# Masked products by one expert in the first token stage, work moved across the seams between stages, narrower causal masks and another order in the second attention

## The chip, the cores and the metric

One NeuronCore of a Trainium2 chip runs the whole program. The metric is the device time in microseconds of one execution, the median of several. The engines are PE (matmul), DVE (vector), ACT (scalar), POOL (GpSimd) and SP, which here only issues DMAs. In the code `nc.tensor` work is under `@block.tensor`, POOL's under `@block.gpsimd`, and so on.

## What is computed

Two layers, each an attention and a gated expert block on the same normalised input, over 4 batches of 1024 tokens of 128 values. The reference, cut:

```python
# layer 0: xn = layernorm(x); x = x + attention0(xn) * silu(experts0(xn))
scores = (Q K^T + Q rel_emb^T) / sqrt(8)          # 16 heads of 8, relative positions clipped to +-127
out = softmax(scores) V;  out Wo + bo
onehot = one_hot(argmax(xt @ gate_w + gate_b))    # 8 experts, the best one
g = einsum('te,eth->th', onehot, xt @ expert_w + expert_b)
# layer 1: the same frame with
scores = q k^T + causal                            # 16 half heads of 8, -inf above the diagonal
w = attn[:, :, 0] - lam * attn[:, :, 1];  o = rms(w v);  o Wo
hmid = gelu(x w1^T + b1); y = hmid w2^T + b2       # 8 experts, 256 hidden, the best two weighted
```

## The kernel before

The program is four stages: `token_stage(0)`, `attention_stage(0)`, `token_stage(1)`, `attention_stage(1)`. Each stage is one block; at its end all engines meet, and the next stage begins for all. I call them tokens 0, attention 0, tokens 1 and attention 1.

**A token stage** takes 8 groups of 512 tokens. For a group it loads X (POOL issues the DMA, L601 and L638), DVE takes mean and variance (`statistics`, L907 to L912), POOL the reciprocal root by three Newton steps (`scale`, L437 to L454), DVE normalises (`normalise`, L917), PE transposes (L832) and ACT copies to XT (L738). Then come the projections Q, K and V (L837, L845, L850), the router, and the split of Q and K into bf16 parts, whose pieces POOL makes (`parts`, L613 and L616) and SP stores to DRAM. `steps` writes the order out by hand: in eight steps the expert work of group g alternates with the front work of group g+1, and the functions named `body` of all engines walk it in the same order.

The expert work of tokens 0 is masked. PE spreads the one-hot choice of an expert over all partitions (`spread_choice`, L797, a 128x512 matmul with the weight `pick_e`), DVE multiplies it with XT into HM (L1015), and PE multiplies HM with the expert's weight into one accumulating bank (L809). This goes by two experts: two spreads, one product of 1024 columns, eight matmuls. The semaphores are `cb_psum` (spread done), `xm_ready` (product done) and `cb_used` (bank read). In the first group DVE also makes the tables of the attention (`attention_tables`) at the odd experts.

After the eighth expert ACT takes the activation into G (L729), and SP stores G to DRAM (L678). SP ends a token stage by waiting until all its stores have landed, `g_stored` last (L713).

**An attention stage** takes 32 units of 128 queries (8 a batch). Its order on each engine comes from a planner, `attention_plan`: it lists the steps of all units with costs (`COST`) and what they wait for, and takes for each engine, among the steps that could start within `NEAR_BY` ns of the earliest one, the one with the least due time (`AIM`, in units; a step that keeps PE's shape is favoured by `STAY`). Per unit PE makes scores once for the row maxima (`row_scores` L1191 in layer 1, `max` and `near` in layer 0), DVE reduces them (L1448), PE transposes the maxima (L1369), POOL splits them in three bf16 rows, and SP puts these into QS beside the queries (L1208). Then PE makes scores again with the maxima subtracted (`far_scores`, L1178), ACT takes exp (L1306), and PE multiplies with V (L1388). Three double banks are shared by both kinds of scores. In layer 0 the blocks beside the diagonal go through `near_scores` (L1153, L1158), for which POOL first copies the unit's queries from QS into QN and QP (step `perm`, L1255 and L1256).

In layer 1 a block on the diagonal is masked by adding -1e30 with matmuls (`mask_rows`, L1167): the weight is one half of the identity, the moving side one half of the mask's rows, repeated for four heads. A unit has four such masks, two for its maxima and two for its exponentials.

At the start of an attention stage ACT issues the DMAs for the keys of batch 1 (`load_kv`, L473 to L477), and those of batches 2 and 3 after the last output copy of units 7 and 15. POOL loads the residual and G of a unit (L1241, L1242).

## Time and profile before

| | us |
|---|---|
| median of 3 runs | 2071.6 (2067.59 to 2082.31) |
| profiled execution | 2077.91 |
| its span, first to last instruction | 2076.1 |
| PE busy in the span | 1767.2 (85%) |
| DVE busy | 1325.2 (64%) |
| ACT busy | 1195.4 (58%) |
| POOL busy | 1146.4 (55%) |

Busy time is the union of an engine's instructions. Idle time in a row is what stood just before the instruction or group, with the instruction that ended it behind the arrow. The stages follow each other without overlap, so a microsecond taken from one is a microsecond of the program unless a later stage gives it back.

### The profile page before, as it was taken

The numbers are of one execution on the slowest core, as the hardware profiler recorded it, in microseconds if no ns is written. First come the engines' busy times: TensorE is split into PE (matmuls) and PEld (weight loads), VectorE is DVE, ScalarE is ACT, GpSimd is POOL, SyncE is SP. The second block draws the span as 40 slices with busy tenths as digits, with TensorE's granted clock in tenths as the row PEclk, the third lists the DMA queues.
The fourth block names the chain that finished last, engine by engine and source line by source line (L and its number), as shares of the span: only waits on it lengthen the run. The fifth ranks groups of instructions, "written<-read, shape, count | busy, mean of one in ns | idle before, by whom it ended". The sixth has DMA issues, their size and how long they took to land. (4 is left out here: it accounts for less than half of the span.)

```text
span 2076.1 us, 78586 instructions
## 1 busy us (share of the span) xinstructions
PE 1767.2 (85%) x34080; PEld 1327.7 (64%) x34080; DVE 1325.2 (64%) x1965; ACT 1195.4 (58%) x1438; POOL 1146.4 (55%) x1502
## 2 busy tenths in 40 slices
PE   5887489998898998989999759999968978879886
PEld 4666377777777776778877536666735545546554
DVE  5442367777676766877777424445467868867883
ACT  2322167777677766777877623344416645656555
POOL 4742469997699858998898621221112333333433
PEclk9887699999999999999999869999979989979998
DMA  3456312123221241222121121133220131121110
GB/s 104 129 146 191 93 52 66 48 65 96 73 65 59 67 106 60 68 68 59 55 62 55 52 91 53 57 95 88 80 61 18 30 66 26 41 52 30 26 26 16
DMA packets 166300, 139.97 MB, mean 67 GB/s; under 512 B 91715, under 2 KB 157014, under 8 KB 160454
## 3 DMA queue, kind: packets, MB, share of 16 engines
q1 hardware_dynamic: 153370, 105.93, 17.9%
q10 hardware_dynamic: 7212, 16.42, 3.3%
q0 software_dynamic: 5376, 12.59, 2.2%
q8 instruction: 271, 4.44, 0.9%
q14 instruction: 71, 0.58, 0.1%
HBM read 90.98 MB, written 43.12 MB: 65 GB/s over the span
## 5 line engine op out<-in xcount | busy, mean ns | idle before, releaser
L1306 ACT ACTIVATE a_EX<-bank 128x1024 f32<-128x1024 f32 x624 | 616.1, 1025 | 292.4 <-PE bank L1178 227.4
L1425 DVE TENSOR_TENSOR a_PM<-bank,a_PM 128x1024 f32<-128x1024 f32 x336 | 402.2, 1222 | 169.0 <-PE bank L1178 156.8
L1265 POOL TENSOR_TENSOR a_SN<-a_SN,a_MB 128x1024 f32<-128x1024 f32 x176 | 421.1, 2429 | 46.3 <-DMA a_MB<-m_dram 45.1
L1448 DVE TENSOR_REDUCE a_M<-bank 128x2 f32<-128x1024 f32 (+3 forms) x304 | 340.3, 1165 | 85.5 <-PE bank L1191 54.9
L1388 PE MATMUL bank<-a_EX,VV 128*32 128x128 f32 x9984 | 360.0, 288 | 3.5 <-issue 1.8
L1178 PE MATMUL bank<-QS,KS 51*128 51x128 bf16 (+1 forms) x4992 | 237.9, 230 | 89.5 <-DMA QS<-a_MP 38.1
L1388 PEld LDWEIGHTS bank<-a_EX,VV 128*32 128x32 f32 x9984 | 270.8, 115 | 52.1 <-issue 22.9
L1178 PEld LDWEIGHTS bank<-QS,KS 51*128 51x128 bf16 (+1 forms) x4992 | 160.1, 100 | 183.1 <-issue 57.6
L1302 ACT ACTIVATE a_SN<-bank 128x1024 f32<-128x1024 f32 x176 | 177.2, 1026 | 93.6 <-PE bank L1158 92.5
L1310 ACT ACTIVATE a_SN<-a_SN 128x1024 f32<-128x1024 f32 x176 | 185.4, 1058 | 38.8 <-POOL a_SN L1265 38.5
L1158 PE MATMUL bank<-QP,rel_t 112*128 112x32 bf16 x5632 | 197.7, 177 | 1.4 <-issue 1.2
L1158 PEld LDWEIGHTS bank<-QP,rel_t 112*128 112x128 bf16 x5632 | 170.5, 97 | 2.0 <-issue 1.9
L1153 PE MATMUL bank<-QN,KS 112*128 112x64 bf16 x2816 | 142.6, 194 | 27.7 <-POOL QP L1256 20.7
L1026 DVE SCALAR_TENSOR_TENSOR t_ACC<-bank,t_C,t_ACC 128x128 f32<-128x128 f32 x256 | 72.1, 345 | 147.4 <-PE bank L825 146.4
L1178 PE MATMUL bank<-QS,KR 48*128 48x128 bf16 (+1 forms) x2688 | 126.1, 229 | 38.0 <-DVE a_PM L1425 15.7
L825 PEld LDWEIGHTS bank<-t_w,t_HM 128*128 128x128 f32 x1024 | 122.1, 192 | 47.2 <-ACT t_HM L723 29.5
L1191 PE MATMUL bank<-KS,QS 48*128 48x128 bf16 (+3 forms) x1152 | 117.3, 288 | 34.1 <-DVE a_M L1448 21.7
L1178 PEld LDWEIGHTS bank<-QS,KR 48*128 48x128 bf16 (+1 forms) x2688 | 82.2, 99 | 82.4 <-issue 36.5
L825 PE MATMUL bank<-t_w,t_HM 128*128 128x128 f32 x1024 | 127.2, 278 | 8.4 <-ACT t_HM L723 6.9
L1432 DVE TENSOR_TENSOR a_PM<-a_SN 128x1024 f32<-128x1024 f32 x64 | 106.9, 1671 | 42.2 <-ACT a_SN L1302 36.0
L1256 POOL COPY QP<-QS 48x1024 bf16<-48x1024 bf16 x64 | 131.5, 2054 | 0.0
L1153 PEld LDWEIGHTS bank<-QN,KS 112*128 112x128 bf16 x2816 | 107.2, 98 | 35.7 <-issue 33.4
(151 smaller groups left out, 2487.8 us busy)
## 6 DMA issues: line engine op xcount, KB each, us to landing
a_MB<-m_dram SPq DMA_DIRECT2D x32, 1024.0 KB, 4.9
QS<-q_dram SPq DMA_DIRECT2D x192, 96.0 KB, 3.0
KS<-k_dram ACTq DMA_DIRECT2D x12, 768.0 KB
q_dram<-t_PARTS SPq DMA_DIRECT2D x32, 192.0 KB, 2.8
k_dram<-t_PARTS SPq DMA_DIRECT2D x16, 384.0 KB, 2.9
QS<-a_MP SPq DMA_DIRECT2D x384, 2.0 KB
q_dram<-t_PARTS SPq DMA_DIRECT2D x32, 128.0 KB, 2.6
k_dram<-t_PARTS SPq DMA_DIRECT2D x16, 256.0 KB, 2.9
```

Source lines behind the costliest of these rows:

```text
L825: last = pe.matmul(y, HM[:, k % 2, h, t * P:(t + 1) * P], w2[:, k, h, :], start=h == 0, stop=h == 1)
L1153: pe.matmul(out_b[:, :, 4 * pair:4 * pair + 4], KS[0:KD, it.u // NB % 2, pair, it.jb * P:(it.jb + 1) * P], QN[:, r, pair, q0:q0 + CQ // 2, ...
L1158: last = pe.matmul(out_b[:, i, :], rel_t[:, y:y + P], QP[:, r, q0 + i, :, :].rearrange("k h a -> k (h a)"), start=False, stop=i == CQ // 2 ...
L1178: last = pe.matmul(bank[:, 2 * it.n + hh, k * P:(k + 1) * P], kblock(hh, rows, it.u, it.jb, pair), QS[hh * HALF:hh * HALF + rows, it.u % Q ...
L1256: last = pool.tensor_copy(QP[rows, r, :, :, a], QS[rows, q, :, :, :].rearrange("k p h (q b) -> k q (p h) b", b=2)[:, :, :, a])
L1265: pool.tensor_tensor(near_view(sn), near_view(sn), as_near(MB[:, :, :], it.part), ALU.add)\
L1302: act.activation(near_buffer(u, jb)[:, part, :], src.rearrange("p b c -> p (b c)"), ACT.Copy).then_inc(act_done, 1)
L1306: act.activation(as_banks(EX[:, it.need % ER[layer]], part), by_head, ACT.Exp, scale=SCALE).then_inc(act_done, 1)
L1310: act.activation(sn, sn, ACT.Exp, scale=SCALE).then_inc(nexp_done, 1)
L1388: last = pe.matmul(dst_o, VV[:, u // NB % 2, jb, vo:vo + 32], ex, start=bool(it.first) and h < 4, stop=bool(it.last), skip_group_check=True)
L1425: dve.tensor_tensor(pm, mb.rearrange("p hh (k i) -> p hh k i", k=4), pm, ALU.max).then_inc(max_used, 1)
L1448: dve.tensor_reduce(target.rearrange("p (hh k) -> p hh k", hh=2)[:, :, p0:p0 + g], mb[:, :, 0:g * width].rearrange("p hh (k j) -> p hh k j ...
```

## The change

It has five parts.

1. Tokens 0: the masked products are made by one expert in place of two. A spread, a product of 512 columns and the handshake are each for one expert; the first four spreads of a group are issued in front steps 6 and 7, and expert k issues the spread of expert k + 4.
2. Seam 1: POOL copies the queries of units 0 and 1 (`permute`) at the end of tokens 0. ACT's exponential and DVE's last steps for `lam` move into attention 0.
3. Seam 2: in attention 0 POOL loads the first X of layer 1 and SP its projection weights into a part of KR that is free by then, after unit 28's output; DVE takes the statistics after the output of unit 30, POOL the root before unit 31's addition, and DVE normalises before unit 31's output.
4. The end of both token stages no longer waits for the stores of G; the loads of G in the attention wait for what they read, and the first copy into OS, which now shares its place with G, waits for all stores.
5. Attention 1: a mask is built from tables of 64 shifted key columns in two halves. Each of its four matmuls has 256 columns in place of 512 and writes every second column of its bank. The cost of a mask in the planner falls from 480 to 260, and layer 1 has new due times and windows, so that its order changes. The order of attention 0 stays, but for the moved copies.

The diff, cut to its core:

```diff
-        "mask": 480, "evict": 1028, ...
+        "mask": 260, "evict": 1028, ...
...
-    {"max": (-0.94, 0.96), "mrow": (-5.54, -2.26), "msplit": (-1.51, -3.76), "exp": (1.3, 0.81),
+    {"max": (-0.89, 0.93), "mrow": (-5, -1.11), "msplit": (-2.16, -1.22), "exp": (1.31, 0.71),
...
-NEAR_BY, STAY = (179, 222), (0.55, 1.3)
+NEAR_BY, STAY = (179, 493), (0.55, 0.47)
...
+        spare = KR[:, 0, :, :].rearrange("p a s -> p (a s)").bitcast(F32)
+        X1 = spare[:, 0:512].rearrange("p (t d) -> p t d", d=P)
+        XN1 = spare[:, 512:1536].rearrange("p (c t d) -> p c t d", c=2, d=P)
...
                     parts(GROUPS - 1)
+                    if layer == 0:
+                        for u in range(NR):
+                            permute(pool, u)
...
-                    sp.wait_ge(g_stored, 16 * GROUPS + 1)
...
                     def spread_choice(g, e):
-                        pe.wait_ge(cb_used, g * (E // 2) + e // 2 + 1)
-                        for k in range(2):
-                            last = pe.matmul(bank[:, HB + e % 4 + k, :], pick_e[:, e + k, :], CTB[:, :], start=True, stop=True)
-                        last.then_inc(cb_psum, 1)
+                        pe.wait_ge(cb_used, g * E + e + 1)
+                        pe.matmul(bank[:, HB + e % 4, :], pick_e[:, e, :], CTB[:, :], start=True, stop=True).then_inc(cb_psum, 1)
...
-                            if k % 2 == 0:
-                                if k + 2 < E:
-                                    spread_choice(f, k + 2)
-                                pe.wait_ge(xm_ready, f * (E // 2) + k // 2 + 1)
+                            pe.wait_ge(xm_ready, f * E + k + 1)
+                            if k + 4 < E:
+                                spread_choice(f, k + 4)
...
-                        if kind == "front" and k == 7 and layer == 0:
-                            spread_choice(f, 0)
+                        if kind == "front" and k >= 6 and layer == 0:
+                            spread_choice(f, 2 * (k - 6))
+                            spread_choice(f, 2 * (k - 6) + 1)
...
-                        if kind == "expert" and layer == 0 and k % 2 == 0:
-                            dve.wait_ge(cb_psum, f * (E // 2) + k // 2 + 1)
+                        if kind == "expert" and layer == 0:
+                            dve.wait_ge(cb_psum, f * E + k + 1)
                             if f or k >= 4:
-                                dve.wait_ge(y_psum, f * E + k - 2)
-                            dve.tensor_tensor(HM[:, k // 2 % 2, :, :], bank[:, HB + k % 4:HB + k % 4 + 2, :],
-                                              XT[:, p:p + 1, :].broadcast_to([P, 2, GROUP]), ALU.mult).then_inc(cb_used, 1)
+                                dve.wait_ge(y_psum, f * E + k - 3)
+                            dve.tensor_tensor(HM[:, k // 2 % 2, k % 2, :], bank[:, HB + k % 4, :], XT[:, p, :],
+                                              ALU.mult).then_inc(cb_used, 1)
...
             def mask_rows(pe, it, which):
-                for part in range(2):
+                for half in range(2):
                     for hh in range(2):
                         rows = slice(hh * HALF, (hh + 1) * HALF)
-                        last = pe.matmul(bank[:, 2 * it.n + hh, :].rearrange("p (h c) -> p h c", h=4), mask_b[rows, 0, part, :],
-                                         mask_b[rows, which, part, None, :].broadcast_to([HALF, 4, P]), start=False,
-                                         stop=part == 1, skip_group_check=True)
+                        out_h = bank[:, 2 * it.n + hh, :].rearrange("p (h c a) -> p h c a", h=4, a=2)[:, :, :, half]
+                        last = pe.matmul(out_h, mask_b[rows, which, half * P:(half + 1) * P],
+                                         mask_b[rows, which, None, 2 * P:].broadcast_to([HALF, 4, HALF]), start=False, stop=True,
+                                         skip_group_check=True)
...
                         elif it.kind == "final":
+                            if layer == 0 and u == UNITS - 1:
+                                scale(pool, 1, 0)
...
+                            if layer == 0 and u == UNITS - 4:
+                                pool.wait_ge(av_done, spare_free)
+                                for r in range(2):
+                                    pool.wait_ge(stored[r], 16 * GT // 2)
+                                load_x(pool, 1, dst, X1, 0)
...
+                    if layer == 0:
+                        act.wait_ge(lam_sum, 1)
+                        act.activation(lam_s[:, 0:2], lam_s[:, 0:2], ACT.Exp).then_inc(lam_exp, 1)
...
+                            if layer == 0 and u == UNITS - 1:
+                                normalise(dve, 1, X1, XN1, 0, 0)
...
+                            if layer == 0 and u == UNITS - 2:
+                                statistics(dve, 1, X1, 0)
```

What this makes of PE's order in tokens 0, from the last matmuls of one group's bias (`out_b`) to the values of the next (`t_pick_e` is a spread, `t_exp_w` the matmuls of an expert, `t_XN` the transposition, `t_wq`, `t_wk` and `t_wv` the projections). Before:

```order
L864 MATMUL bank<-out_b,t_CT 128x128 x4
L809 MATMUL bank<-t_exp_w,t_HM 128x128 x4
L797 MATMUL bank<-t_CTB,t_pick_e 128x512 x4
L809 MATMUL bank<-t_exp_w,t_HM 128x128 x4
L832 MATMUL bank<-eye,t_XN 128x128 x4
L809 MATMUL bank<-t_exp_w,t_HM 128x128 x4
L837 MATMUL bank<-t_XT,t_wq 128x512
L840 MATMUL bank<-gate_w,t_XT 128x8 x4
L797 MATMUL bank<-t_CTB,t_pick_e 128x512 x2
L809 MATMUL bank<-t_exp_w,t_HM 128x128 x4
L845 MATMUL bank<-t_XT,t_wk 128x512
L809 MATMUL bank<-t_exp_w,t_HM 128x128 x4
```

After, from the same matmuls on:

```order
L923 MATMUL bank<-out_b,t_CT 128x128 x4
L858 MATMUL bank<-t_CTB,t_pick_e 128x512 x2
L868 MATMUL bank<-t_exp_w,t_HM 128x128 x4
L858 MATMUL bank<-t_CTB,t_pick_e 128x512 x3
L868 MATMUL bank<-t_exp_w,t_HM 128x128 x4
L891 MATMUL bank<-eye,t_XN 128x128 x4
L858 MATMUL bank<-t_CTB,t_pick_e 128x512
L868 MATMUL bank<-t_exp_w,t_HM 128x128 x4
L896 MATMUL bank<-t_XT,t_wq 128x512
L899 MATMUL bank<-gate_w,t_XT 128x8 x4
L858 MATMUL bank<-t_CTB,t_pick_e 128x512
L868 MATMUL bank<-t_exp_w,t_HM 128x128 x4
```

Two spreads have moved ahead of the last expert of the group, and the others stand one by one between the experts; none is left between the values and the fifth expert.

POOL at seam 1, from the last split of Q and K on (the BRANCH rows are the change of stage, `a_XG` the loads of residual and G). Before:

```order
L616 TENSOR_TENSOR t_PARTS<-t_FR,t_PARTS 128x1536
L598 UNCONDITIONAL_BRANCH
L1235 UNCONDITIONAL_BRANCH
L1241 DMA a_XG<-in_x 128x128
L1242 DMA a_XG<-g_dram 128x128
L1241 DMA a_XG<-in_x 128x128
L1242 DMA a_XG<-g_dram 128x128
L1255 COPY QN<-QS 48x512x2
L1256 COPY QP<-QS 48x1024
```

After:

```order
L522 COPY QN<-QS 48x512x2
L523 COPY QP<-QS 48x1024
L665 UNCONDITIONAL_BRANCH
L1275 UNCONDITIONAL_BRANCH
L1282 DMA a_XG<-in_x 128x128
L1283 DMA a_XG<-g_dram 128x128
L1282 DMA a_XG<-in_x 128x128
L1283 DMA a_XG<-g_dram 128x128
L522 COPY QN<-QS 48x512x2
L523 COPY QP<-QS 48x1024
```

The copies of units 0 and 1, four pairs of which the last is shown, now stand ahead of the change of stage; the pair behind the loads is that of unit 2.

PE in attention 1 around the transposed maxima of unit 9 (`eye,a_M`), before the keys of batch 2 are loaded (this load follows the `a_EX,VV` row, the last one of unit 7). Before:

```order
L1369 MATMUL bank<-eye,a_M 16x128
L1178 MATMUL bank<-QS,KS 128x128 x8
L1167 MATMUL bank<-mask_b 128x512 x4
L1178 MATMUL bank<-QS,KS 128x128 x8
L1167 MATMUL bank<-mask_b 128x512 x4
L1191 MATMUL bank<-KS,QS 128x128 x8
L1402 MATMUL bank<-eye,a_OF 128x128
L1191 MATMUL bank<-KS,QS 128x128 x8
L1388 MATMUL bank<-a_EX,VV 32x128 x16
```

After:

```order
L1411 MATMUL bank<-eye,a_M 16x128
L1228 MATMUL bank<-KS,QS 128x128 x8
L1204 MATMUL bank<-mask_b 128x256 x4
L1444 MATMUL bank<-eye,a_OF 128x128
L1228 MATMUL bank<-KS,QS 128x128 x16
L1447 MATMUL bank<-wo,a_OT 128x128
L1228 MATMUL bank<-KS,QS 128x128 x8
L1204 MATMUL bank<-mask_b 128x256 x4
L1430 MATMUL bank<-a_EX,VV 32x128 x16
```

The exponentials' scores of unit 8 (`QS,KS` with their masks) have moved ahead of the transposition, and row scores of the next unit (`KS,QS`) stand in their place.

## Rows read from the trace of the kernel before

**Rows 1.** Busy time by stretch: start:end, length, each engine, then PEclk, DMA share, GB/s.

```profile
core 0: us, PE busy (x) PEld busy (x) DVE busy (x) ACT busy (x) POOL busy (x), PEclk, DMA share, GB/s
0.00:216.00 216.00, 159.65 (x864) 125.50 (x864) 95.86 (x265) 60.72 (x76) 96.42 (x141) 0.83 0.50 142
216.00:1205.00 989.00, 862.85 (x22816) 715.80 (x22816) 681.16 (x608) 699.49 (x784) 790.56 (x528) 0.93 0.23 65
...
1522.00:2076.00 554.00, 460.11 (x8832) 286.46 (x8832) 409.61 (x556) 314.80 (x385) 198.04 (x704) 0.90 0.16 36
```

**Rows 2.** Timeline of PE, a middle group: start, length, instruction, idle before and releaser.

```profile
119.11 1.41 PE L809 MATMUL bank<-t_exp_w,t_HM 128*128 128x128 f32 x8 [0.93 <-DVEq L1017]
...
127.21 1.05 PE L809 MATMUL bank<-t_exp_w,t_HM 128*128 128x128 f32 x8
128.73 1.16 PE L850 MATMUL bank<-t_wv,t_XT 128*128 128x128 f32 x8 [0.47 <-ACT t_FQ L747]
...
132.34 0.82 PE L809 MATMUL bank<-t_exp_w,t_HM 128*128 128x128 f32 x5 [1.92 <-DVEq L1017]
```

**Rows 3.** DVE: three rows of the timeline, one of the groups (count, busy, mean ns).

```profile
28.00 2.62 DVE L985 TENSOR_SCALAR t_rel_r<-t_rel_f 112x766 f32<-112x766 f32 x1
...
127.03 0.22 DVE L956 COPY t_C<-t_OH 128x32 f32<-128x32 f32 x1 [0.38 <-issue]
...
131.02 1.23 DVE L1015 TENSOR_TENSOR t_HM<-bank,t_XT 128x1024 f32<-128x1024 f32 x1 [0.20 <-issue]
...
L925 DVE TENSOR_SCALAR t_FQ<-bank 128x512 f32<-128x512 f32 x16 | 10.9, 683 | 2.2 <-PE bank L845 2.2
```

**Rows 4.** Timeline at seam 1, POOL, ACT, ACT's queue and PE.

```profile
213.32 1.28 ACT L775 ACT_TABLE_LOAD   x1
...
216.59 0.60 POOL L1241 DMA_DIRECT2D a_XG<-in_x  x1 [16.95 <-POOLq L598]
...
219.72 0.47 ACTq L477 DMA_DIRECT2D VV<-v_dram  x1
...
230.22 1.04 POOL L1255 COPY QN<-QS 48x1024 bf16<-48x1024 bf16 x1 [8.51 <-issue]
...
233.28 0.59 PE L1153 MATMUL bank<-QN,KS 112*128 112x64 bf16 x8 [20.69 <-POOL QP L1256]
...
242.63 1.02 ACT L1302 ACTIVATE a_SN<-bank 128x1024 f32<-128x1024 f32 x1 [0.24 <-PE bank L1158]
```

**Rows 5.** Timeline at seam 2, POOL, DVE and PE.

```profile
1205.16 0.77 POOL L601 DMA_DIRECT2D t_X<-x_mid  x1 [2.45 <-POOLq L1198]
...
1208.87 0.87 DVE L907 BATCH_NORM_STATS2 t_stats<-t_X 128x6 f32<-128x128 f32 x4 [6.73 <-DMA t_X<-x_mid]
...
1216.47 1.09 PE L832 MATMUL bank<-eye,t_XN 128*128 128x128 f32 x4 [14.67 <-DVE t_XN L917]
...
1220.74 0.87 DVE L907 BATCH_NORM_STATS2 t_stats<-t_X 128x6 f32<-128x128 f32 x4 [4.42 <-DMA t_X<-x_mid]
```

**Rows 6.** Timeline at seam 3, SP's queue and PE.

```profile
1519.29 0.36 SPq L678 DMA_DIRECT2D g_dram<-t_G  x1
...
1522.24 0.61 PE L1191 MATMUL bank<-KS,QS 48*128 48x128 bf16 x8 [6.10 <-PEq L598]
```

**Rows 7.** The masks: the line's matmuls, the chain's shares, two rows of the timeline.

```profile
L1167 PE MATMUL bank<-mask_b x512: 373/377/631, 1522.6 to 2054.7; 64*128 64x512 bf16 x171
...
by line: DVE a_M L1448 5.9%; issue 3.4%; PE bank L1388 3.3%; PE bank L1178 2.5%; PE bank L1191 1.6%; DMA QS<-a_MP 1.4%; PE bank L1167 1.3%; ACT a_EX L1306 1.0%; DVEq L1494 0.6%; SPq L1208 0.5%; PE bank L1396 0.4%; PE bank L1402 0.4%; PE ban
...
1551.37 0.60 PE L1167 MATMUL bank<-mask_b 64*128 64x512 bf16 x4
1551.80 0.39 PE L1191 MATMUL bank<-KS,QS 48*128 48x128 bf16 x8
```

**Rows 8.** Timeline of attention 1, rows of maxima, keys of batch 2, PE's wait.

```profile
1672.24 4.30 SPq L1208 DMA_DIRECT2D QS<-a_MP  x6
...
1674.12 1.49 ACTq L473 DMA_DIRECT2D KS<-k_dram  x2
...
1688.71 1.04 PE L1178 MATMUL bank<-QS,KS 51*128 51x128 bf16 x16 [8.13 <-DMA QS<-a_MP]
```

More of the change, by code:

```diff
@@ L1112, in attention_stage @@
             AV, MISC = 2 * SLOTS2, 2 * SLOTS2 + 1
+            far_end = max(n for n, it in enumerate(plan["pe"]) if it.kind in ("max", "exp") and it.u < UNITS - NB)
+            spare_free = min(it.k for it in plan["pe"][far_end:] if it.kind == "av") + 1
             def block_of(u):
@@ L1181, in far_scores @@
                 if masked:
-                    last = mask_rows(pe, it, 2)
+                    last = mask_rows(pe, it, 0)
                 return last
```

198 lines of the change are left out of this document (111 added, 87 removed).

## The prediction

> **What bounds the kernel now.** I read the busy time by stage first [rows 1]. The program is four stages in a row, each ended by a barrier of all engines: tokens 0 (0 to 216 us), attention 0 (to 1205), tokens 1 (to 1522) and attention 1 (to 2076). Inside attention 0 PE is busy 862.85 of 989 us at a granted clock of 0.93, and the change leaves its order on PE, ACT and DVE alone, so I expect it to keep its length and only to start sooner. The change works in four places: the expert steps of tokens 0, the three seams between stages, and the masks and the order of attention 1. I take them in this order, from the timeline of each.
>
> **Tokens 0, the products by one expert.** In a middle group PE waits twice for DVE's masked product: 0.93 us before the first expert and 1.92 us before the fifth; the 0.47 us before the values is for ACT [rows 2]. The first wait is the chain spread, product, expert: the spread for experts 0 and 1 is issued right ahead. After the change the spread for 0 and 1 stands one expert earlier, so product 0 is ready before PE asks: -0.9 us. The second wait stands behind DVE's evacuation of the values: product at 131.02, 1.23 us long, PE at 132.34. A product of 512 columns costs about 0.68 us, the mean of the nearest row (a 128x512 operation out of PSUM) [rows 3], so PE starts 0.55 us sooner; but the two spreads that lay in this wait now stand at the group's end, on PE's path, and take about 0.5 us. That is 0. Against this, the product for the fourth expert used to be made with the third, ahead of the routing chain; now it stands behind it. Routing ends at 127.03 + 0.22 = 127.25 [rows 3]; with 0.68 for the product and 0.2 for the handover PE could start this expert at 128.1, where it started at 127.21 [rows 2]. Of these 0.9 us the wait for ACT hides 0.47: +0.4. Sum -0.5 us a group, six groups with this pattern: -3. In the first group four table steps of DVE stand ahead of the odd products; the first of them alone takes 2.62 us [rows 3] and was covered by the product for two experts made before it. Cover gone, I walk through this group and end 1.3 us later. The last group has no front steps; PE runs there without waiting for DVE. Sum: -2 us. Bounds: -8 if fewer stops also lift the clock (0.83 over the stage [rows 1]), +6 if the tables cost their full length.
>
> In rows, the extra work of DVE is 32 more operations: 2 x 0.68 for one of 1.23 is 0.13, and the pause before the next product is 0.20 [rows 3], together 0.33 us, or 10.6 us in all. I take it as hidden, since DVE is busy only 95.86 of 216 us [rows 1]. The Trainium skill speaks against this edit: "VectorE: DVE Perf Modes", Rules for kernel authors, asks to minimize the number of operations, and its section on the TRN2 errata gives (N + 151) / 0.96 ns for an fp32 tensor_tensor, an estimate of 691 ns at 512 and 1224 ns at 1024. The row of 1.23 us agrees; two small ones would cost 0.16 us more than one large, and by that rule alone the edit would be a loss of 32 x 0.16 = 5 us.
>
> **Seam 1, tokens 0 to attention 0.** POOL's last work in tokens 0 ends at 216.59 - 16.95 = 199.64; it is then idle until the next stage, where it copies QS for units 0 and 1, and PE cannot begin before the first unit is copied: PE starts at 233.28, after 20.69 us idle [rows 4]. In this chain POOL stands still for 8.51 us (put down to issue) between the two halves of unit 0. The change puts both units' copies right behind 199.64. The half that began at 230.22 released PE at 233.28, 3.06 us [rows 4]; four halves take 12.2: 211.9. The landing of the last store of G, which the barrier waited for, is no longer waited for. So the stage starts near 212.5 where it started near 216. PE then begins the near scores at once. ACT must first issue the keys' DMAs, done at 219.72 + 0.47 = 220.2 or 4.2 us after the start, and then take its exponential with a table load of 1.28 us [rows 4], so it evicts from 218.3 on. From PE's start to the end of the sixth eviction it was 242.63 + 1.02 - 233.28 = 10.4 us [rows 4], which gives 212.8 + 10.4 = 223.2; ACT's late start adds about 2 with three slots to fill: 225.5 for 243.65. That is 18 us. Units 2 and on may stumble over the same 8.51 us, but they come later than unit 0 did. Term: -18. Bounds: -14 (the pause and the loads of the new stage now meet the first near scores) to -20 (from 233.28 straight to 213).
>
> **Seam 2, attention 0 to tokens 1.** Now X is loaded after the barrier (issued 1205.16), normalised by DVE, POOL and DVE, and PE begins at 1216.47, 14.67 us after its last work [rows 5]. After the change this has all been done inside attention 0, ahead of the last unit's output, where DVE and POOL wait for others; I cost it at 0. Uncovered it would be the stretch from 1208.87 to 1216.47 [rows 5], 7.6 us. PE can begin 0.3 us after the barrier: -11. But DVE takes the second X before it evacuates the first projection. That load waited for the first X to be free and was used from 1220.74. Issued right at the stage's start it lands, like the first (1208.87 - 1205.16 = 3.7 us [rows 5]), at about 1209.5, 11.2 sooner; the expert weights are in flight beside it, for which I give up 0.7 us: -10.5. Bounds: -8 to -16, if PE's clock also stays up.
>
> **Seam 3, and the wait for the last store.** The last G of tokens 1 is issued at 1519.29; the next stage begins at 1522.24 [rows 6]. Without that wait the stage starts at about 1520.3: -2.
>
> **Attention 1, masks.** A mask is four matmuls of 512 columns, 128 masks in 512 matmuls [rows 7]. From the start of one mask to the next instruction is 1551.80 - 1551.37 = 0.43 us (two run side by side on separate rows). With 256 columns it is 0.215 us, 27.5 us less over 128 masks. The chain of waits puts 1.3% of the span, 27 us, on this line, in an order where DVE's maxima hold 6% [rows 7]; halved, 13.5. DVE is busy 409.61 of 554 us [rows 1] and will take some of it back: -10. Bounds 0 and -27.5. That the results are written to every second column is not priced by any row; the near scores write runs of four and I see no cost there, so I take none.
>
> **Attention 1, the new order.** The order differs in small shifts: PE takes the ninth unit's maxima and its transposed product in another sequence. The worst stall there is one PE wait of 8.13 us for the rows of maxima: SP issues these rows at 1672.24, over 4.30 us, and at 1674.12 ACT issues the next keys, and the late rows queue behind them [rows 8]. It comes twice. In the new order the unit's rows still have about the same lead, short of what six issues need. I take 0, with 8 us to either side.
>
> **Sum.** -2 - 18 - 10.5 - 2 - 10 = -42.5 us. The profiled execution took 2077.9 us (span 2076.1), which gives 2035.4. It lies 6.3 above the median of the three runs, 2071.6, and so the median should be 2071.6 - 42.5 = 2029 us.
>
> **The rivals.**
> - Attention 1 gives more: PE, not DVE, is what ends last there (PE busy 460.11 of 554 us [rows 1]), all 27.5 us of the masks come off, and the new order frees the rows before the keys' loads. Then -60: 2012 us. For it: the stall of rows 8 is a matter of about 2.5 us of lead. Against: long runs of maxima where DVE never rests. Chance 0.18.
> - The handshakes land on the path: tokens 0 ends 10.6 us later than it would (32 x 0.33) and not 2 sooner, so -30: 2042 us. For it: DVE holds product and routing in one queue, and the tables of the first group. Against: its idle time. This is also what the page's rule asks for, at 5 us: 2036. Chance 0.08.
> - A seam is paid back: attention 0 starts 18 us sooner but unit 2's copies, which wait for the near scores and then for POOL's 8.51 us, hold it, and only the 3.5 us of the barrier and some 4 more stay. Then -32: 2040 us. Chance 0.08.
> - Slower than before: the masks' writes to every second column run slowly. It decides when they eat 42.5 - 10 = 32 us: half of 128 masks are on the chain, so 0.5 us for each, a mask of 0.93 instead of 0.43 us. Nothing in the rows shows such a write. For over 1% slower it would need 1.26 us a mask. Chance 0.02.
> - The forecast: 0.64.
>
> **How the numbers follow.** The likeliest is 2029. Its bounds from the terms taken together are about 2015 to 2043; the rival of attention 1 reaches to 2008 and the two repayments to 2042, so 2008 to 2046 leaves out about 2 in 10. A measurement of this kernel tells about 1% (20.7 us) from no change: faster means below 2050.9. The forecast and the first three rivals lie there but for a tail of 0.07, and of the last one 0.02 is slower: 0.92, 0.06, 0.02.
>
> **What would show it.** Right: in tokens 0 no wait of PE for DVE before the first expert of a group, one of about 0.5 us before the fourth, DVE products near 0.69 us; POOL's copies right behind its last split; PE's first near score within 2 us of the stage's start and near 213; PE's first transposition of tokens 1 less than 1 us after the barrier; masks of 0.21 us. Wrong: tokens 0 longer by more than 5 us; attention 0 longer by more than 5 us from its first near score; a mask as long as before; PE waits for maxima rows that are longer than 8 us or more than two.

## The result and the profile after

The change makes the kernel 0.6% faster: 2065.4 us median of 20 runs (2056.1 to 2082.5) against 2079.7 us of 20 runs of the kernel before (2067.6 to 2085.9), ratio 0.9938 with a 95% interval of 0.9919 to 0.9956. That is 14 us where 42.5 were forecast; the time lies above the forecast's range of 2008 to 2046, and above the 2050.9 below which the prediction called the kernel faster. Of the 36 us between 2029 and 2065.4, 8 are not the change's: the forecast started from a median of three runs, 2071.6, and twenty runs of the same kernel have 2079.7. The profiled executions are 2062.2 (span 2060.4) against 2077.9, 15.7 us apart.

Busy time by stage of the changed kernel, in the columns of [rows 1]; the stages are cut where their barriers fall:

```profile
0.00:222.90 222.90, 164.41 (x864) 125.34 (x864) 102.51 (x295) 59.29 (x74) 107.55 (x149) 0.84 0.48 136
222.90:1190.40 967.50, 859.68 (x22816) 712.24 (x22816) 689.93 (x623) 700.75 (x786) 774.75 (x534) 0.94 0.23 68
1190.40:1498.60 308.20, 284.63 (x1568) 200.09 (x1568) 136.35 (x523) 120.32 (x193) 57.75 (x115) 0.95 0.27 77
1498.60:2060.40 561.80, 458.63 (x8832) 288.44 (x8832) 411.02 (x556) 315.41 (x385) 196.72 (x704) 0.91 0.15 36
```

Tokens 0 takes 223 us and not 216, and attention 1 takes 562 us and not 554, though its masks should have become cheaper. Both are longer where the forecast had them shorter. The two stages between carry the gain.

**Tokens 0.** In the middle groups the forecast pattern is there (timeline, PE and DVE, one middle group): no wait ahead of the first expert, 0.49 us ahead of the fourth, 1.92 us ahead of the fifth as in [rows 2], and products of 0.69 us:

```profile
130.42 1.16 PE L868 MATMUL bank<-t_exp_w,t_HM 128*128 128x128 f32 x8
...
136.99 0.69 DVE L1056 TENSOR_TENSOR t_HM<-bank,t_XT 128x512 f32<-128x512 f32 x1
137.83 0.37 PE L858 MATMUL bank<-t_CTB,t_pick_e 8*128 8x512 bf16 x1 [0.49 <-DVEq L1058]
...
142.10 3.18 PE L868 MATMUL bank<-t_exp_w,t_HM 128*128 128x128 f32 x16 [1.92 <-DVEq L1058]
```

The first group is another matter. DVE's table steps (L1030 to L1041) now stand ahead of the product that PE needs next:

```profile
39.45 1.01 DVE L1030 SCALAR_TENSOR_TENSOR t_rel_f<-t_rel_p,levels,t_rel_r 112x766 f32<-112x766 bf16 x1
40.53 1.43 DVE L1032 CAST t_rel_p<-t_rel_f 112x766 bf16<-112x766 f32 x1
...
42.03 0.69 DVE L1056 TENSOR_TENSOR t_HM<-bank,t_XT 128x512 f32<-128x512 f32 x1
42.87 0.37 PE L858 MATMUL bank<-t_CTB,t_pick_e 8*128 8x512 bf16 x1 [3.07 <-DVEq L1058]
...
48.37 1.02 DVE L1034 SCALAR_TENSOR_TENSOR rel_t<-t_rel_p,levels,t_rel_f 112x766 bf16<-112x766 bf16 x1
...
50.77 0.69 DVE L1056 TENSOR_TENSOR t_HM<-bank,t_XT 128x512 f32<-128x512 f32 x1
51.57 2.08 PE L868 MATMUL bank<-t_exp_w,t_HM 128*128 128x128 f32 x8 [1.16 <-DVEq L1058]
```

From PE's transposition for the second group (30.99) to that for the third (64.25) it takes 33.3 us; before it took 24.2 (29.84 to 54.08). PE waits 3.07, 1.92 and 1.16 us in it, 6.15 us together; before, its six waits in the same stretch made 6.42. So the waits have moved and have not grown: the 9 us are slower matmuls. The eight matmuls of an expert take 1.16 us in some places and 2.08 in others, and six of the eight experts in this stretch take 1.9 us or more, where it was one before:

```profile
32.63 2.08 PE L868 MATMUL bank<-t_exp_w,t_HM 128*128 128x128 f32 x8
...
37.78 1.16 PE L868 MATMUL bank<-t_exp_w,t_HM 128*128 128x128 f32 x8
...
62.38 2.08 PE L868 MATMUL bank<-t_exp_w,t_HM 128*128 128x128 f32 x8
```

From 44 us on the granted clock is 0.50 (windows under e1). At 32.63 the matmuls are as slow, ahead of the first long wait, and there the column reads 1.00. The next group takes 25.8 us (21.6), the three after it 21.0, 20.3 and 20.2 (23.1, 21.5 and 23.0).

**Seam 1.** The copies stand right behind POOL's last split, as forecast, but that split itself is 10 us later than before (206.67 against 196.54), and SP's stores of the last projections and of G follow from it:

```profile
206.67 3.10 POOL L678 TENSOR_TENSOR t_PARTS<-t_FR,t_PARTS 128x1536 bf16<-128x1536 f32 x1 [5.21 <-ACT t_PARTS L835]
...
209.80 4.53 SPq L730 DMA_DIRECT2D q_dram<-t_PARTS  x6
...
218.51 4.10 SPq L744 DMA_DIRECT2D g_dram<-OS  x2
...
221.59 0.60 ACT L794 ACTIVATE OS<-bank 128x512 f32<-128x512 f32 x1 [13.02 <-DMA g_dram<-OS]
...
223.34 0.59 PE L1189 MATMUL bank<-QN,KS 112*128 112x64 bf16 x8 [5.77 <-PEq L665]
```

PE's first near score comes at 223.34 (233.28 before), right at the stage's start; ACT's sixth eviction ends at 235.37 (243.65).

**Seam 2.** PE transposes 3.25 us after its last work, where it was 14.67 [rows 5]. The second X, issued at 1191.76, is used at 1199.41, 7.65 us later. DVE's evacuations for PE stand behind it, so that PE waits 4.77 us for the first of them (before: 1.13, at 1222.96):

```profile
1191.52 1.09 PE L891 MATMUL bank<-eye,KR 128*128 128x128 f32 x4 [3.25 <-DVEq L941]
1191.76 0.81 POOL L485 DMA_DIRECT2D KR<-x_mid  x1 [0.41 <-issue]
...
1199.41 0.87 DVE L490 BATCH_NORM_STATS2 stats<-KR 128x6 f32<-128x128 f32 x4 [10.81 <-DMA KR<-x_mid]
...
1201.64 2.07 PE L904 MATMUL bank<-t_XT,KR 128*128 128x512 f32 x2 [4.77 <-DVE t_FQ L966]
```

**Masks.** The line's matmuls (durations min/median/max, first and last start) and, from the timeline, one mask with what follows it; compare [rows 7]:

```profile
L1204 PE MATMUL bank<-mask_b x512: 377/417/712, 1499.2 to 2038.5; 64*128 64x256 bf16 x171
...
1529.10 0.60 PE L1204 MATMUL bank<-mask_b 64*128 64x256 bf16 x4
1529.63 1.08 PE L1430 MATMUL bank<-a_EX,VV 128*32 128x128 f32 x32
```

Each matmul is half as wide and no shorter. The time from a mask's start to the value matmul behind it is 0.53 us, in the kernel before too (1552.03 to 1552.56); to a score it is 0.39 to 0.43, where it was 0.43.

### The profile page after: what moved, and what is told of

Read it like the earlier page. It is cut to its first block and busy times, and to the rows that moved or that the text cites. A ratio compares the mean times of both kernels' runs of the same rounds, so it can differ in the third digit from the quotient of the medians.

```text
span 2060.4 us, 78711 instructions
## 1 busy us (share of the span) xinstructions
PE 1767.4 (86%) x34080; PEld 1326.1 (64%) x34080; DVE 1339.8 (65%) x1997; ACT 1195.8 (58%) x1438; POOL 1136.8 (55%) x1502
## 5 line engine op out<-in xcount | busy, mean ns | idle before, releaser
L852 PE MATMUL bank<-t_XT,t_w 128*128 128x512 f32 x256 | 123.9, 608 | 0.0
```

## The experiments

All runs are cut at four marks: the end of ACT's sixth eviction in attention 0 ("sixth"), the length of attention 0 from there to PE's last output, the stretch from that output to the first row score of attention 1 (tokens 1 with its seams), and attention 1 from there to the end. "Tables" is where DVE's table steps stand in the first group of tokens 0, ahead of or behind the product by one expert, or "pairs" where a product is for two experts. Each line is one profiled execution; the median is that of its timed runs (their number in brackets), the ratio is against the kernel before in the same call.

| run | tables | sixth | att. 0 | tokens 1 | att. 1 | median (runs) | ratio (95%) |
|---|---|---|---|---|---|---|---|
| before | pairs | 243.7 | 958.2 | 320.4 | 553.9 | 2079.7 (20) | |
| e5 before again | pairs | 240.8 | 954.0 | 320.1 | 551.8 | 2068.6 (1) | |
| after | ahead | 235.4 | 952.9 | 310.5 | 561.6 | 2065.4 (20) | 0.9938 (0.9919 to 0.9956) |
| e6 after again | ahead | 234.3 | 964.8 | 310.9 | 562.0 | 2073.8 (1) | |
| e11 after again | ahead | 228.1 | 962.0 | 310.6 | 558.0 | 2062.4 (8) | 0.9936 (0.9914 to 0.9958) |
| e1 tables behind | behind | 224.7 | 961.3 | 311.2 | 561.9 | 2062.0 (6) | 0.9927 (0.9904 to 0.9949) |
| e2 order of before | ahead | 232.9 | 959.4 | 310.2 | 553.9 | 2061.8 (10) | 0.9924 (0.9893 to 0.9955) |
| e3 pairs | pairs | 226.5 | 958.9 | 311.1 | 564.2 | 2063.2 (7) | 0.9925 (0.9902 to 0.9949) |
| e4 masks side by side | ahead | 229.6 | 965.9 | 310.7 | 549.3 | 2057.0 (4) | 0.9899 (0.9866 to 0.9933) |
| e7 both mended | behind | 226.0 | 967.8 | 310.1 | 554.7 | 2055.0 (6) | 0.9871 (0.9833 to 0.9908) |
| e10 both mended again | behind | 229.4 | 959.1 | 310.4 | 553.6 | 2054.1 (6) | 0.9889 (0.9866 to 0.9913) |
| e12 pairs, order of before | pairs | 225.6 | 958.3 | 310.2 | 552.8 | 2049.1 (6) | 0.9871 (0.9840 to 0.9903) |
| e8 half the keys | behind | 221.4 | 942.9 | 310.3 | 545.2 | 2021.6 (1) | |
| e9 late keys | behind | 223.1 | 960.2 | 310.1 | 547.6 | 2044.6 (6) | 0.9838 (0.9815 to 0.9862) |
| e14 pairs, late keys | pairs | 225.7 | 957.6 | 310.4 | 545.9 | 2046.0 (6) | 0.9864 (0.9836 to 0.9891) |
| e13 price of a mask | ahead | 234.0 | 959.2 | 310.3 | 599.5 | 2102.2 (4) | 1.0128 (1.0089 to 1.0167) |

### e1: the tables behind the products

```diff
-                        if kind == "expert" and layer == 0 and k % 2 == 1 and f == 0:
-                            attention_tables(k)
...
                             dve.sem_inc(xm_ready, 1)
+                            if k % 2 == 1 and f == 0:
+                                attention_tables(k)
```

> The changed kernel, with one edit: in the first group of tokens 0 each of DVE's four table steps stands behind the masked product of its odd expert, not ahead of it. Theory A (the tables ahead of the odd products hold PE, and the slow clock that follows holds the second group too): the first transposition of the second group to that of the third, 33.3 us now, falls to about 24 (before: 24.2), the next from 25.8 to about 22, POOL's last split starts near 195 instead of 206.67, and the time falls by 9 to 12 us against the changed kernel, to about 2050 us in a profile. Theory B (the 32 handshakes of DVE and PE cost 0.33 us each, wherever the tables stand): at most 3 us come back, the groups keep 33 and 26 us within 3.

The first group falls from 33.3 to 25.5 us, the second from 25.8 to 22.9, POOL's last split starts at 195.74, PE's first near score comes at 212.49, and the sixth eviction ends at 224.73: theory A, by its marks. The median fell by only 3.4 us against the changed kernel, where theory A said 9 to 12; by that mark it stays undecided, as the executions scatter by more (below). Where the 8 us of the first group come from is seen in the windows of the first group (columns as in rows 1). The changed kernel:

```profile
29.00:44.00 15.00, 11.85 (x50) 8.60 (x50) 10.56 (x26) 5.51 (x6) 10.95 (x18) 0.99 0.45 132
44.00:57.00 13.00, 9.92 (x44) 8.77 (x43) 7.55 (x20) 1.06 (x2) 2.71 (x2) 0.50 0.14 43
57.00:65.00 8.00, 8.00 (x31) 5.66 (x30) 4.32 (x12) 1.48 (x1) 5.30 (x8) 0.50 0.10 21
```

and the same stretches of e1:

```profile
29.00:44.00 15.00, 12.31 (x71) 9.43 (x71) 12.47 (x33) 5.52 (x6) 11.11 (x17) 1.00 0.42 123
44.00:57.00 13.00, 9.58 (x50) 7.12 (x49) 11.40 (x25) 2.55 (x3) 7.41 (x5) 0.71 0.18 54
57.00:65.00 8.00, 6.90 (x34) 4.58 (x32) 3.72 (x13) 2.34 (x4) 5.70 (x15) 0.84 0.71 213
```

With the tables ahead PE does 50 matmuls in the first 15 us and not 71, and then runs 21 us at a granted clock of 0.50, its lower level of 1.2 GHz. Its waits in this group make 6.1 us in e1 too, so here as well it is the pace that changed: two of the eight experts are slow and not six.

Of six profiled executions with the tables ahead five had 31.8 to 33.3 us in this group, and one (e11) had 26.3. With the tables behind all five (e1, e7 to e10) had 25.5 to 26.8. So the tables' place brings the slow pace in most executions, and e11 shows that it need not. Which pause brings it stays open. In the last two windows the clock is 0.50 or 0.51 in the first profile, e2 and e4, 0.68 and 0.71 in e6 and e13, which take the same 32.4 us, and 0.71 and 0.84 in e11. e6 and e13 were slow earlier: until 42 us e6 takes 2.08 us for each of its experts, again where the column reads 1.00.

### e2 and e4: the order of before, and masks that write side by side

e2 takes back the planner's numbers for attention 1, and keeps the new masks:

```diff
-        "mask": 260, "evict": 1028, ...
+        "mask": 480, "evict": 1028, ...
...
-NEAR_BY, STAY = (179, 493), (0.55, 0.47)
+NEAR_BY, STAY = (179, 222), (0.55, 1.3)
```

with layer 1's due times of before.

> The changed kernel, with the five plan rows of attention 1 and the mask's cost of before, so that attention 1 has the order of before and only its masks are the new ones. Theory A (the new order costs 7.7 us, by six waits for late rows of maxima in place of three): attention 1 from its first matmul to the end takes 554 us again, where the changed kernel takes 561.6, and PE waits 18 us for the rows of maxima and not 27. Theory B (the new masks, or the stage's new start against the transfers, cost it): 560 us or more stay.

Attention 1 takes 553.9 us, to the tenth what it took in the kernel before. So the new order costs all of the 8 us, and the new masks bring nothing. The median is 3.6 us below that of the changed kernel. The waits of PE for the rows of maxima (total, times, longest), the changed kernel over attention 1:

```profile
PE bank L1215 <- DMA QS<-a_MP: 26.7, 6, 9.6
```

and e2:

```profile
PE bank L1215 <- DMA QS<-a_MP: 19.0, 5, 8.6
```

The changed kernel waits 9.59 and 9.42 us where the kernel before has 8.13 ([rows 8]) and 8.31, and has further waits at 1633.10 (1.55), 1966.42 (1.65) and in the last unit, 2029.45 (3.35), where nothing can take them back. The first of the two long ones:

```profile
1656.85 4.07 SPq L1245 DMA_DIRECT2D QS<-a_MP  x6
...
1658.90 1.58 ACTq L547 DMA_DIRECT2D KS<-k_dram  x2
...
1671.53 0.61 PE L1215 MATMUL bank<-QS,KS 51*128 51x128 bf16 x8 [9.59 <-DMA QS<-a_MP]
```

The rows are issued 2.05 us ahead of the keys, as before (1.88), and PE goes on 14.7 us behind their issue (16.5). What changed is when PE asks for them: it stands idle from 5.1 us behind the issue, where it was 8.3. The second wait is alike (5.1 and 8.0 us).

e4 differs from e2 in one line; the masked columns are then the wrong ones:

```diff
-                        out_h = bank[:, 2 * it.n + hh, :].rearrange("p (h c a) -> p h c a", h=4, a=2)[:, :, :, half]
+                        out_h = bank[:, 2 * it.n + hh, :].rearrange("p (h a c) -> p h a c", h=4, a=2)[:, :, half, :]
```

> The kernel of e2 (changed kernel, attention 1 in the order of before), and the masks' matmuls write their 4 x 64 results to neighbouring columns instead of to every second one; the mask then lands on wrong columns, so the scores of attention 1 are wrong and only its time counts. Theory A (the write to every second column takes two cycles a column and eats what the halved width should give): one mask takes 0.21 us to the next instruction where it takes 0.43 in both kernels, and attention 1 is 10 us shorter than in e2 (bounds 0 and 27). Theory B (the time of a mask is set by something else: its weights, its pieces of 64 columns, the broadcast read): a mask stays at 0.43 us and attention 1 at the length of e2.

The mask's row and one mask with its follower in e4:

```profile
L1204 PE MATMUL bank<-mask_b x512: 267/271/418, 1506.6 to 2033.9; 64*128 64x256 bf16 x171
...
1557.79 0.38 PE L1204 MATMUL bank<-mask_b 64*128 64x256 bf16 x4
1558.01 0.39 PE L1215 MATMUL bank<-QS,KS 51*128 51x128 bf16 x8
```

It is 0.22 us to the next instruction, at the same granted clock (1.00), the same widths and the same 64-column pieces. Theory A: these matmuls, which write f32 results to every second column of PSUM, take twice as long a column. Halved masks are worth 4.6 us of attention 1 (549.3 against 553.9, one execution each; the stage has 552.8 to 554.7 in the four with this order and the strided masks). That is half of the 10 that I took, here and in the prediction, and less than a fifth of the 27.5 that the masks would lose in sum.

### e3 and e12: pairs in tokens 0

The edit takes the expert-by-one products back and keeps all else: in `spread_choice` two matmuls and one handshake, in DVE's body one product of two experts.

```diff
-                            dve.tensor_tensor(HM[:, k // 2 % 2, k % 2, :], bank[:, HB + k % 4, :], XT[:, p, :],
-                                              ALU.mult).then_inc(cb_used, 1)
+                            dve.tensor_tensor(HM[:, k // 2 % 2, :, :], bank[:, HB + k % 4:HB + k % 4 + 2, :],
+                                              XT[:, p:p + 1, :].broadcast_to([P, 2, GROUP]), ALU.mult).then_inc(cb_used, 1)
```

> The changed kernel, with the masked products of tokens 0 for two experts at once again (one product of 1024 columns, spreads in pairs, one handshake for two). Theory A (the seam between tokens 0 and attention 0 is worth the 18 us that were forecast, and only tokens 0 spoils it): POOL's last split starts at 196.5, attention 0 starts near 212.5, ACT's sixth eviction ends near 225.5 (changed kernel: 235.4), and the time falls by about 10 us. Theory B (the seam itself is worth less, since ACT's loads of the keys and the last store of G hold the start wherever tokens 0 ends): the sixth eviction ends at 232 or later, and the time falls by less than 4 us. By the middle groups alone, which are 1.4 to 2.8 us shorter with single products, pairs would lose some 9 us of what the first group gives.

The first near score comes at 210.16 and the sixth eviction ends at 226.48: by these marks the seam is worth what was forecast, and tokens 0 spoilt it. The median does not show it: 2063.2 us is 2.2 below the changed kernel, where theory A said 10 and theory B less than 4. e12 is e3 with the order of before in attention 1.

> The changed kernel with products for two experts at once (as e3) and the order of before in attention 1 (as e2): what is left of the change without the expert-by-one products. Theory A (with its tables out of the way the product by one is worth about what the middle groups show, 1 to 2 us each): e7 and e10 are 3 to 8 us faster than this. Theory B (what the middle groups gain the first group and the handshakes eat, and the two are the same): within 3 us. In e1 and e3 the first near score came at 212.49 and 210.16, which speaks for B.

e12 has 2049.1 us against 2055.0 and 2054.1 of e7 and e10. So the single products are not 3 to 8 us faster, as theory A has it; the 5 us by which they are slower are more than theory B's 3, and e14 below speaks on them. The sixth eviction ends at 226.5, 225.6 and 225.7 with pairs (e3, e12, e14), and at 224.7, 226.0, 229.4 and 223.1 with single products and the tables behind: means of 225.9 and 225.8. What the middle groups gain, some 1 us each (20.3, 20.2 and 20.8 in e1; 21.3, 22.0 and 20.9 in e3), the first two groups lose.

### e5, e6, e10, e11: how much one execution says

> The kernel before, once more, for a second profile. Theory A (the length of attention 0 is drawn anew in each execution by the two waits of PE for rows of maxima that meet the loads of the next keys, at the eighth and the sixteenth unit, 0 to 10 us each; attention 1 is fixed): attention 0 from ACT's sixth eviction to PE's last output is within 958 plus or minus 8 us and moves with these two waits, and attention 1 takes 553.9 us within 0.5 again. Theory B (each stage is fixed by its order): attention 0 takes 958.2 us within 1.

> The changed kernel, once more. Theory A (as for the kernel before): attention 1 takes 561.6 us within 0.5 again, tokens 0 has its first two groups at 32 to 33 and 26 us again, and attention 0 is longer than the 952.9 us of the first profile, since that one had a short wait (2.5 us) at the sixteenth unit: 955 to 962. Theory B (starting sooner changes nothing in it): 952.9 within 1.

> The changed kernel again, as the base of this call: 2065 us within 3, attention 1 at 561.6 within 0.5, tokens 0 with its first two groups at 32 to 33 and 26 us.

Attention 1 came back at 551.8 (553.9) in the kernel before and at 562.0 and 558.0 (561.6) in the changed one, so it is not fixed to half a microsecond, but the two kernels stay apart. Attention 0 is drawn anew: 952.9, 964.8 (above the 955 to 962 expected) and 962.0 us in three executions of the changed kernel. A part of this lies at two places, PE's waits for the rows of maxima at the eighth and the sixteenth unit, which follow a load of keys: none and 2.5 us in the first profile of the changed kernel (2.1 one unit after the eighth), 4.8 and 9.1 in e6, 10.0 and 7.1 in e4, 9.1 and 9.0 in e10. They are not all of it: e10, with 18.2 us in the two, has 959.1 us in the stage, and e7, with 4.0 and 8.4, has 967.8. e11 is also the execution with the better clock in the first group; my expectation of 32 to 33 us there was wrong.

### e7 and e10: both losses mended

The edits of e1 and e2 together.

> The changed kernel with the tables behind the products (e1) and the order of before in attention 1 (e2). Theory A (both losses are real and add, and e1's small median gain came from scatter in attention 0): ACT's sixth eviction ends near 225, attention 1 takes 554 us, and the median falls by 10.6 + 7.7 = 18 us against the changed kernel, of which some 3 may stay in attention 0: 2047 to 2052. Theory B (attention 0 gives back what an earlier start brings): the median falls by no more than 8 us, to 2057 or above.

> The kernel of e7 again, beside the changed kernel and the kernel with pairs on one chip. Both losses real: 10 to 18 us below the changed kernel of this call; the first attempt gave 10.4. If it is less than 5 us, e7 was scatter.

e7 has 2055.0 us, 10.4 below the changed kernel's 20 runs; e10 has 2054.1, 8.3 below e11 of the same call, where 10 to 18 were expected. By the stages it should be 14 (6.5 at the sixth eviction, 7.7 in attention 1). The gain is real and its size lies between the theories; the 4 to 6 us that lack are no more than what six runs with a spread of 9 to 19 us leave open.

### e8 and e9: the keys and the rows of maxima

```diff
-                        eng.dma_start(KS[rows, b % 2, :, :].rearrange("r p t -> r (p t)"), src).then_inc(kv_in[layer][b % 2], 16)
+                        cut = PAIRS * S // (2 if b else 1)
+                        eng.dma_start(KS[rows, b % 2, :, :].rearrange("r p t -> r (p t)")[:, 0:cut], src[:, :, 0:cut])\
+                           .then_inc(kv_in[layer][b % 2], 16)
```

> The kernel of e7, and of each load of keys but the first only half the columns are loaded (384 KB in place of 768 KB each; the other half of the keys is left as it was, so scores and output are wrong and only its time counts). Theory A (rows of maxima that SP issues right behind a load of keys wait for the keys' bytes, which are ahead of them in the same DMA engines): the waits at the eighth and sixteenth unit fall to about half, from 8 us to 3 or 4 in attention 1, which ends 8 us sooner than in e7. Theory B (the rows are late because SP issues them late and one by one): the waits in attention 1 stay at 8 us.

PE's two long waits in attention 1 are 5.44 and 4.75 us (8.46 and 8.26 in e7) and the stage is 9.5 us shorter; in attention 0 the sixteenth unit's wait is 1.32 us, the eighth has none over 1, and the stage is 18 us below the mean of the others. This is one execution, and in attention 1 theory A holds: the rows' lateness grows with the bytes of the keys. e9 keeps all bytes and issues them later:

```diff
                             act.activation(as_banks(EX[:, it.need % ER[layer]], part), by_head, ACT.Exp, scale=SCALE).then_inc(act_done, 1)
+                            if owed is not None and u > owed:
+                                load_kv(layer, act, owed // NB + 2)
+                                owed = None
...
                             if u % NB == NB - 1 and u // NB + 2 < B:
-                                load_kv(layer, act, u // NB + 2)
+                                owed = u
```

> The kernel of e7, and ACT issues each next load of keys (the four after the first two of each attention stage's own) not at the last copy of a unit but behind the first exponential of the next one, that is when this unit's rows of maxima have landed. Theory A (the rows are held by the keys' bytes, and that alone sets both the two waits of 8.3 us in attention 1 and the scatter of attention 0): the waits of PE at units 8 and 16 fall below 2.5 us in both stages, attention 1 takes about 542 us in place of 554.7, attention 0 at most 956, the median falls by 12 to 22 us against e7 and scatters less. Theory B (the keys only meet the next thing: POOL's loads and its pause of 10 us, and the next rows): the median falls by less than 5 us.

In attention 1 no wait for the rows of maxima over 1 us is left, where e10 has 8.48 and 8.61. The stage is 6.0 us shorter and not 12. The waits of PE in attention 1 show where the rest went; e10:

```profile
PE bank L1215 <- DMA QS<-a_MP: 18.1, 3, 8.6
PE bank L1444 <- POOL a_OF L1313: 13.0, 6, 7.7
PE bank L1215 <- ACT a_EX L1346: 8.0, 18, 0.7
```

and e9:

```profile
PE bank L1448 <- POOL a_OF L1313: 18.2, 8, 7.7
PE bank L1215 <- ACT a_EX L1347: 11.1, 19, 1.5
```

It is 5 us more for POOL's normalised output and 3 more for ACT's exponentials. In attention 0 the keys came almost where they had been (726.10 against 729.99 in e10, in a stage that began 6.3 us sooner), the wait of the sixteenth unit stayed at 6.66 us and the stage at 960.2: there theory A was wrong about the remedy. At 2044.6 us (ratio 0.9838) e9 is the version with the lowest median that computes all, 21 us below the changed kernel. It is 10.4 us below e7 and 9.5 below e10 of the same call, which lies between theory B's 5 and theory A's 12, and its runs spread by 10.6 us, no less than e10's 9.4. e14 is e9 with pairs.

> Pairs in tokens 0, the order of before in attention 1 (both as e12), and the keys issued late (as e9): the parts that the runs so far speak for, together. If the gains are apart from each other, 2049.1 - 10 = 2039 us, below e9 (2044.6) by 5; if the 5 us between e12 and e10 were scatter, it equals e9 within 3. Attention 1 takes 547.6 us within 1 as in e9.

The median is 2046.0 us, the same as e9 within 3: by this expectation the 5 us between e12 and e10 were scatter, and products by one or by two are the same here. Attention 1 takes 545.9 us, 0.7 less than the least that was expected.

### e13: the planner's price of a mask alone

```diff
-        "mask": 260, "evict": 1028, ...
+        "mask": 480, "evict": 1028, ...
```

> The changed kernel with the planner's price of a mask at 480 ns again, the other new numbers of attention 1 kept (start times, NEAR_BY, STAY). Theory A (the price of 260 ns, which the masks don't have, is what spoils the order): attention 1 falls from 561.6 to about 554 us. Theory B (the loss is in how the order's numbers fell out and not in this price): attention 1 stays above 558 us or gets longer, since the other numbers were chosen beside 260.

Attention 1 takes 599.5 us, 38 more than with 260; the waits of PE there:

```profile
PE bank L1215 <- DMA QS<-a_MP: 36.8, 5, 15.3
```

Theory B: the wrong price is not the loss by itself, since the other numbers were chosen beside it. One number of the planner moves the stage by 38 us. The rows of maxima are 10 of them (26.7 us in the changed kernel). The two long waits, 15.35 and 14.95 us, are of another kind than those above: here the order issues the rows 11.7 and 12.1 us behind the keys, and PE stands idle 4.5 us before they are issued. Another 10 us are PE's waits for DVE's maxima (51.7 against 41.7 us), and PE is busy 14 us longer (472.8 against 458.6) at a granted clock of 0.88 in place of 0.91.

## Why the prediction was wrong

**Tokens 0, -2: wrong.** The step that failed is "Cover gone, I walk through this group and end 1.3 us later." Over six executions with the tables ahead the sixth eviction ends at 232.4 on average, with pairs at 225.9: +6.5 us, where the term was -2 with a bound of +6. The walk counted waits, and these came out no longer than before (6.15 us in the first profile against 6.42). What it put at nothing is the pace of the matmuls: six of the group's eight experts at half pace, with a granted clock of 0.50 for 21 us in the profiled execution. That the tables' place brings this on is shown by e1 and e7 to e10; how it does so stays open. The rest of the term held: no wait before the first expert, 0.49 before the fourth, and the middle groups about 1 us shorter. Expert by expert is worth nothing in sum even when the tables are out of its way (225.8). The rule of the Trainium skill that was weighed there, "VectorE: DVE Perf Modes", Rules for kernel authors, gave a loss of 5 us for the small products; the product's 0.69 us is what its formula gives, but with the tables behind no loss is seen. That DVE's idle time hid it is my reading; no run shows it apart. The rival "handshakes on the path" named its condition, one queue for tables and product, and its price of +10.6 was nearer than mine, yet its cause was not the handshakes: e1, e7, e9 and e10 keep all 32 of them and lose the 6.5 us.

**Seam 1, -18: right in size.** With pairs the sixth eviction moves from 242.2 (two executions of the kernel before) to 225.9, -16.3, within -14 to -20; e1's 224.7 and its near score at 212.49 meet the forecast of 225.5 and near 213. The changed kernel itself shows 10 us of it, as the late tokens 0 pushes POOL's split, SP's stores and the barrier along. No run takes back the moved copies or the dropped wait for G alone, so how the 16 us divide between them is not shown.

**Seams 2 and 3, -12.5: half a step too good.** Measured -9.8 (320.3 to 310.5). The wait for PE fell by 11.4 us and the last seam by 1.8, as forecast. The failed step is the second X that lands "like the first" after 3.7 us: it took 7.65 beside the weights' loads, for which 0.7 us had been given, and PE's wait behind it grew from 1.13 to 4.77 us. That the weights held it is argued from their place (SP issued 1 MB of them 0.6 us ahead of X, where the kernel before issued them 0.9 us behind its first X); no run moves them.

**Masks, -10: wrong, and 0 was the bound.** "That the results are written to every second column is not priced by any row ... so I take none." The stride doubles the time of a column (e4) and takes back just what half the columns save. Nor would a faster mask have given 10 us: in e4 it gave 4.6. The price that the slow rival set as its point of decision (0.93 us a mask) was not reached, but its mechanism is the one at work: a mask stays at 0.39 to 0.43 us.

**The new order, 0 within 8: at the bound.** Attention 1 is 7.7 us longer than with the order of before (means of five and four executions, 561.5 and 553.8). The place was right, the rows of maxima beside the keys, and "about the same lead" held (2.05 us for 1.88). What the step left out is when PE asks for the rows: 3 us sooner behind their issue, so that it waits 1.1 to 1.5 us longer twice; and new waits of 1.5 to 3.4 us came, one of them in the last unit.

**Attention 0, 0: open.** The two profiles of the kernel before have 958.2 and 954.0 us, eleven of changed ones 960.9 on average (952.9 to 967.8). By the medians less the other stages' means it would be 962 before and 959 after. Two executions are too few, and I can't say whether some 5 us of the earlier start are paid back there; e1 and e3, whose medians fell by 3.4 and 2.2 us for 6.5 at the sixth eviction, would fit it as well as scatter.

**The sum.** By the means of the stages: -9.8 to the sixth eviction, -9.8 over tokens 1, +8.7 in attention 1, together -11, and -14.2 by the medians. Of the 31 us that the stages lack against the forecast of -42.5, about 10 are the masks, 8 the order, 8 the tables with the slow pace, 3 the second X and 2 seam 1. Seam 1 and the middle groups of tokens 0 are the part of the prediction that came out by its mechanism.

## What to carry to other kernels

When one large operation is split in two, look at what stands between the halves in the engine's queue: the second half loses the cover that the first gave it. Here the tables stood there; the consumer's waits moved without growing, but its matmuls ran at half pace for most of the group, and putting the tables behind the product mended it. So read the pace of the matmuls beside the waits, as a walk through the waits alone doesn't show it. Price a narrower matmul with the stride of its output, not only with its columns. Before a planner gets a new cost, measure the operation in the new form, since its other numbers are tuned beside it.

## What the hardware showed beyond that

- Matmuls of 256 bf16 columns with f32 results: 0.22 us for a group of four (two side by side) with results in neighbouring columns (e4), 0.39 to 0.43 us when they go to every second column (changed kernel), and 0.43 us for 512 neighbouring columns (kernel before).
- The same instructions of tokens 0 took 31.8 to 33.3 us in the first group of five executions and 26.3 in a sixth. Over the same 21 us the granted clock was 0.50 or 0.51 in three of them, 0.68 and 0.71 in two and 0.71 and 0.84 in the sixth: the clock's answer to the same work is not the same each time. And the eight matmuls of an expert took 2.08 us, as at 0.50, in a stretch for which the column reads 1.00 (32.63 us, changed kernel).
- Small row loads (2 KB each) issued about 2 us ahead of a load of keys in 768 KB pieces are late with it: PE waited 8.0 to 9.9 us for them in attention 1 (e13, with another lead, aside), and 4.8 and 5.4 with half of the keys' bytes (e8, one execution). With the keys issued later, behind the next unit's first exponential, no such wait over 1.4 us is left there (e9, e14). In attention 0 the same waits came at anything from none to 10 us, and the stage took 952.9 to 967.8 us in one order.
